# An LSTM's x*Wx+b is copied into the gates' PSUM banks by ScalarE, in place of a bf16 split on GpSimd and products by an identity

## What is computed

```
ys = cond / 16
d  = rsqrt(sum_i (ys*ys) (w*w) + 1e-8)
x  = x + ((x * ys) @ w) * d

xW = x @ Wx + b                     # all steps at once
for each step t, with h = cond and c = 0 before the first:
    a = xW[t] + h @ Wh              # 4 gates of 256: i, f, o, g
    c = sigmoid(f) * c + sigmoid(i) * tanh(g)
    h = sigmoid(o) * tanh(c)
    out[t] = x[t] + h
```

## Time and profile before

| | |
|---|---|
| median of 3 executions | 2039.84 us (2039.63 to 2040.46) |
| the profiled execution, its own time | 2039.63 us |
| its span, from the first to the last instruction | 2037.8 us |
| TensorE products | 1993.6 us busy (98%), 59,057 instructions |
| TensorE weight loads | 1771.2 us (87%) |
| VectorE | 1283.8 us (63%) |
| ScalarE | 747.2 us (37%) |
| GpSimd | 623.1 us (31%) |

### The profile page before, as it was taken

How to read it: one execution, slowest core, us unless ns; L and a number is a source line. 1 busy time by engine, 2 the same in 40 slices (tenths; PEclk the granted TensorE clock), 3 DMA queues, 4 the chain that set the end, 5 groups by cost and what they waited for, 6 DMA issues and landing times.

```text
span 2037.8 us, 146916 instructions
## 1 busy us (share of the span) xinstructions
PE 1993.6 (98%) x59057; PEld 1771.2 (87%) x59057; DVE 1283.8 (63%) x8393; ACT 747.2 (37%) x4239; POOL 623.1 (31%) x1800
## 2 busy tenths in 40 slices
PE   8999999999999999999999999999999999999998
PEld 6888888888888888888888888888888888888887
DVE  6666666666666666666666666666666666666665
ACT  3333333333333333333333333333333333333333
POOL 2332333233333323332332333233333323332332
PEclk9555555555555555555555555555555555555555
DMA  2111011111111111111111111111111110111010
GB/s 95 21 21 27 20 20 25 22 20 21 27 20 20 23 24 20 21 27 20 20 21 27 20 20 26 21 20 21 27 20 20 23 24 20 21 27 20 20 21 20
DMA packets 188304, 48.63 MB, mean 24 GB/s; under 512 B 185468, under 2 KB 187784, under 8 KB 188296
## 3 DMA queue, kind: packets, MB, share of 16 engines
...
...
## 4 chain that ended last, share of the span: by engine, by line
PE 91%; DVE 4%; ACT 2%; issue 2%; DMA 1%; SPq 0%; POOL 0%; POOLq 0%; DVEq 0%
PE psum L386 91%; DVE psum L709 3%; ACT scan_in L785 2%; DMA wx_sb<-in_L_cond_Wx_dram 1%; DVE psum L702 1%; DVE wmax L623 0%; SPq L203 0%; POOL wx_sb L315 0%; DVE xt L602 0%; SPq L205 0%; SPq L198 0%; SPq L199 0%; POOLq L61 0%; PE psum L432 0%; POOL y_cols L308 0%
## 5 line engine op out<-in xcount | busy, mean ns | idle before, releaser
L386 PE MATMUL psum<-h_parts,wh_p 128*128 128x2 f16 (+1 forms) x45056 | 1369.1, 166 | 0.0
L386 PEld LDWEIGHTS psum<-h_parts,wh_p 128*128 128x128 f16 x45056 | 1285.1, 104 | 48.3
L386 PE MATMUL psum<-ring,ident_b 128*128 128x4 bf16 (+2 forms) x12288 | 634.3, 168 | 32.8 <-DVE psum L677 2.6
L386 PEld LDWEIGHTS psum<-ring,ident_b 128*128 128x128 bf16 x12288 | 487.7, 105 | 199.2 <-DVE psum L709 179.3
L782 ACT ACTIVATE sig_f<-psum 128x4 f32<-128x4 f32 x1024 | 178.1, 174 | 1035.4 <-DVE psum L700 1035.4
L700 DVE TENSOR_REDUCE psum<-psum 128x4 f32<-128x8 f32 x1024 | 179.0, 175 | 386.7 <-PE psum L386 386.7
L386 PE MATMUL psum<-x_piece,wx_piece 128*128 128x128 bf16 x1536 | 411.0, 268 | 0.0
L287 POOL CAST ring<-xw 128x64 bf16 (+1 forms) x256 | 121.6, 475 | 906.3 <-POOLq L353 906.1
L712 DVE SCALAR_TENSOR_TENSOR h_parts<-scan_h 128x4 f16<-128x4 f32 x1024 | 174.8, 171 | 247.8 <-ACT scan_h L789 247.8
L787 ACT ACTIVATE scan_h<-psum 128x4 f32<-128x4 f32 x1024 | 180.3, 176 | 141.8
L715 DVE TENSOR_TENSOR_SCAN h_parts<-scan_h,h_parts 128x12 f16<-128x12 f32 x1024 | 188.4, 184 | 35.0
...
## 6 DMA issues: line engine op xcount, KB each, us to landing
x_piece<-x_p SPq DMA_DIRECT2D x128, 192.0 KB, 2.7
wx_piece<-wx_p SPq DMA_DIRECT2D x128, 128.0 KB, 2.4
out_dram<-y_rows SPq DMA_DIRECT2D x512, 4.0 KB
...
small_rows<-in_cond_dram SPq DMA_DIRECT2D x1, 2.0 KB
```

What stands on the lines that cost most here:

```text
L386: return nc.tensor.matmul(out_, lhs, rhs, start=first, stop=last, skip_group_check=True)
```

## The change

ScalarE copies x*Wx+b of the next step, in fp32, from `xw` straight to the gates' PSUM banks, and TensorE's h products add to it. Five copies a step: F after the sigmoid of I and G; I, G and O's two chunks after tanh. F, G and O's first chunk have two sums side by side, one for each part of h; each gets half (`share`, a factor of 0.5 in scale and bias of these items when `xw` is made, by `top`, `units`, `bias_s`). The 12 products by the identity, `ring`, and GpSimd's split of `xw` are gone. TensorE waits for the copies by four semaphores of their own (`f_add`, `i_add`, `g_add`, `o_add`). GpSimd's split of x is spread over the first five steps of a turn, each of its instructions after a step's h, and the SP queue waits for `x_split` one turn less. In the last step of a turn the copies are those of the next turn's first step, and their place is worked out there.

```diff
+        ahead_i = banks[I_BANK][:, sums]
+        ahead_f = banks[F_BANK][:, 0:2 * CB].rearrange("p (c q b) -> p c q b", q=2, b=B)
+        ahead_g = banks[G_BANK][:, 0:2 * CB].rearrange("p (c q b) -> p c q b", q=2, b=B)
+        ahead_o = [banks[O_BANK][:, 0:2 * B].rearrange("p (q b) -> p q b", b=B), banks[O_REST][:, 2 * CB:2 * CB + B]]
...
+        f_add, i_add, g_add, o_add = sem("f_add"), sem("i_add"), sem("g_add"), sem("o_add")
...
-                sp.wait_ge(x_split, i + 2)
+                sp.wait_ge(x_split, i + 1)
...
-            def split_rest(half, src):
-
-                nc.gpsimd.tensor_tensor(by_gate(rest[:, :, :]), src, parts(half, 0), ALU.subtract).then_inc(s_pool, 1)
-                settle()
...
-            def split_low(half):
-
-                nc.gpsimd.tensor_tensor(parts(half, 2), by_gate(rest[:, :, :]), parts(half, 1), ALU.subtract).then_inc(ring_full, 1)
...
-            for s, v in last_read("xw"):
-                pool.wait_ge(s, v)
-            pool.wait_ge(s_start, 1)
-            for half in range(2):
-                src = xw_source(half, 0)
-                split_high(half, src)
-                split_rest(half, src)
-                split_middle(half)
-                split_low(half)
...
+                after_step(t + 1)
+                nc.gpsimd.tensor_copy(part[0], now).then_inc(s_pool, 1)
+                settle()
+                after_step(t + 2)
+                nc.gpsimd.tensor_tensor(res, now, part[0], ALU.subtract).then_inc(s_pool, 1)
+                settle()
+                after_step(t + 3)
+                nc.gpsimd.tensor_copy(part[1], res).then_inc(s_pool, 1)
+                settle()
+                after_step(t + HALF)
+                pool.wait_ge(y_turned, i + 1)
                 pool.sem_inc(pool_seen, 1)
-                for half in range(2):
-                    done = t + (half + 1) * HALF
-                    src = xw_source(half, i + 1)
-                    pool.wait_ge(ring_used, 1)
-                    pool.sem_inc(ring_used, -1)
-                    split_high(half, src)
-                    split_rest(half, src)
...
-                    split_low(half)
-                    after_step(done)
...
-                    save(half, t + half * HALF)
-                    if half == 0:
-                        nc.gpsimd.tensor_copy(part[0], now).then_inc(s_pool, 1)
-                        settle()
-                        nc.gpsimd.tensor_tensor(res, now, part[0], ALU.subtract).then_inc(s_pool, 1)
-                        settle()
-                        nc.gpsimd.tensor_copy(part[1], res).then_inc(s_pool, 1)
-                        settle()
-                        nc.gpsimd.tensor_tensor(part[2], res, part[1], ALU.subtract).then_inc(x_split, 1)
+                save(0, t)
+                after_step(t + HALF + 1)
+                nc.gpsimd.tensor_tensor(part[2], res, part[1], ALU.subtract).then_inc(x_split, 1)
+                after_step(t + UNROLL)
+                save(1, t + HALF)
...
-            def input_apart(gate, u, first, last):
-
-                columns = apart(gate, first, last)
-                mm(columns.rearrange("p c q b -> p q c b"), ident_b[:, :],
-                   ring[:, u, gate, 0:2, B * first:B * last].rearrange("p q (c b) -> p q c b", b=B), True, True)
-                return mm(columns[:, :, 0, :], ident_b[:, :], in_ring(gate, u, 2, first, last), False, True)
-
-            def input_together(gate, bank, u, first, last):
-                for part in range(3):
-                    mm_ = mm(together(bank, first, last), ident_b[:, :], in_ring(gate, u, part, first, last), part == 0, True)
-                return mm_
...
-                    if u % HALF == 0:
-                        pe.wait_ge(ring_full, 2 * i + u // HALF + 1)
                     if u == FIRST_PIECE:
                         pe.wait_ge(x_staged, 32 * i + 32)
                         pe.wait_ge(x_read, i + 1)
-                    pe.wait_ge(f_act, t + u + 1)
-                    input_apart(GATE_F, u, 0, K)
                     if u >= FIRST_PIECE:
                         project(done)
                         done += 1
-                    pe.wait_ge(c_done, t + u + 1)
-                    input_apart(GATE_G, u, 0, K)
-                    input_together(GATE_I, I_BANK, u, 0, K)
-                    pe.wait_ge(o_act, t + u + 1)
-                    input_apart(GATE_O, u, 0, 1)
-                    last = input_together(GATE_O, O_REST, u, 1, K)
-                    if u % HALF == HALF - 1:
-                        last.then_inc(ring_used, 1)
                     if u >= FIRST_PIECE:
                         last = project(done)
                         done += 1
                         if done == len(terms):
                             last.then_inc(x_mm, 1)
+                    pe.wait_ge(f_add, t + u + 1)
+                    pe.wait_ge(i_add, t + u + 1)
                     pe.wait_ge(h_hi, t + u + 1)
                     products(GATE_I, I_BANK, 0, 0, K)
                     pe.wait_ge(h_lo, t + u + 1)
                     products_apart(GATE_F, 0, K).then_inc(f_mm, 1)
+                    pe.wait_ge(g_add, t + u + 1)
                     products_apart(GATE_G, 0, K).then_inc(g_mm, 1)
                     products(GATE_I, I_BANK, 1, 0, K).then_inc(ig_in, 1)
+                    pe.wait_ge(o_add, t + u + 1)
                     products_apart(GATE_O, 0, 1).then_inc(o0_mm, 1)
                     products(GATE_O, O_REST, 0, 1, K)
                     products(GATE_O, O_REST, 1, 1, K).then_inc(o_in, 1)
...
+            nc.vector.scalar_tensor_tensor(out=bias_s[:, :], in0=small[:, B * K:NSMALL], scalar=scales[:, 0:1], in1=share[:, :],
+                                           op0=ALU.mult, op1=ALU.mult).then_inc(s_bias, 1)
+            nc.vector.tensor_scalar(top[:, :], share[:, :], scales[:, 0:1], None, ALU.mult).then_inc(s_bias, 1)
+            link(nc.vector.tensor_tensor(x_unit[:, :], scales[:, 0:1], scales[:, 3:4], ALU.mult))
+            nc.vector.tensor_scalar(units[:, :], share[:, :], x_unit[:, :], None, ALU.mult).then_inc(s_bias, 1)
...
+            def in_two(source, gate):
+
+                return source[:, gate * K:(gate + 1) * K, :].unsqueeze(2).broadcast_to([P, K, 2, B])
+
+            def add_f(source):
+                nc.scalar.activation(ahead_f, in_two(source, GATE_F), ACT.Copy).then_inc(f_add, 1)
+
+            def add_i(source):
+                nc.scalar.activation(ahead_i.rearrange("p (c b) -> p c b", b=B), source[:, GATE_I * K:(GATE_I + 1) * K, :], ACT.Copy).then_inc(i_add, 1)
+
+            def add_g(source):
+                nc.scalar.activation(ahead_g, in_two(source, GATE_G), ACT.Copy).then_inc(g_add, 1)
+
+            def add_o(source):
+                first = GATE_O * K
+                nc.scalar.activation(ahead_o[0], source[:, first, :].unsqueeze(1).broadcast_to([P, 2, B]), ACT.Copy)
+                nc.scalar.activation(ahead_o[1], source[:, first + 1, :], ACT.Copy).then_inc(o_add, 1)
+
+            for s, v in last_read("xw") + last_read("x1"):
+                act.wait_ge(s, v)
+            act.wait_ge(s_start, 1)
+            for add in (add_f, add_i, add_g, add_o):
+                add(step_columns(0, 0))
+
             with act.Fori(0, NI) as i:
                 t = i * UNROLL
+                block = act.snap((i // ITEMS) * ITEMS)
+                column = act.snap((i % ITEMS) * UNROLL)
+                next_block = act.snap((((i + 1) % NI) // ITEMS) * ITEMS)
+                next_column = act.snap(((i + 1) % ITEMS) * UNROLL)
                 item = act.snap((i + LEAD) % NI)
                 chunk = act.snap((item // B) % M)
                 for u in range(UNROLL):
@@ -783,16 +746,26 @@
 
                     act.wait_ge(ig_in, both)
                     nc.scalar.activation(sig_ig, pre_ig, ACT.Sigmoid, scale=unscale).then_inc(cell_in, 1)
+                    if u == UNROLL - 1:
+                        act.wait_ge(x_read, i + 1)
+                        source = step_columns(next_block, next_column)
+                    else:
+                        source = step_columns(block, act.snap(column + u + 1))
+                    add_f(source)
                     act.wait_ge(o_in, both)
                     nc.scalar.activation(scan_h[:, :, 1].rearrange("p (h b) -> p h b", b=B), pre_o, ACT.Sigmoid, scale=unscale).then_inc(o_act, 1)
                     act.wait_ge(c_done, step)
                     nc.scalar.activation(scan_h[:, :, 2], cell[:, :, 2], ACT.Tanh).then_inc(t_done, 1)
+                    add_i(source)
+                    add_g(source)
+                    act.wait_ge(o_act, step)
+                    add_o(source)
                     if u == UNROLL - 1:
 
                         act.wait_ge(x_mm, i + 1)
                         act.sem_inc(act_seen, 1)
                         nc.scalar.activation(xw[:, bass.ds(item, 1), :].rearrange("p n t -> p (n t)"), banks[X_BANK][:, 0:P], ACT.Identity,
```

(2 more changed lines are left out.)

58 lines of the change are left out of this document (16 added, 42 removed).

## The result

| | before | after |
|---|---|---|
| median | 2040.15 us (4 executions, 2039.63 to 2040.68) | 2111.97 us (4, 2111.66 to 2112.51) |
| ratio | | 1.0352 (95%: 1.0334 to 1.037) |
| the profiled execution, its own time | 2039.63 us | 2111.66 us |
| its span | 2037.8 us | 2109.9 us |
| first to last of F's sums (L700, now L631) | 1987.12 us | 2057.39 us |

The forecast was 2109, with 2066 to 2128 as its range.

A forecast was written before the change was run, and what follows sets the result against it. The prediction took a chain of 1,024 steps as the bound, with TensorE waiting for h. From 2039.6 us, +61.4 (wait), -13.3 (GpSimd's stall) and +21.1 (ScalarE's copies) gave 2108.8, so 2109 us, range 2066 to 2128.

The forecast's parts named there:

- The wait: Ahead of the h products: waiting for h_hi, i_add and f_add costs 0.06 us more a step, +61.4 us.
- the rival of the cheap wait: Ahead of the h products: the extra wait costs only 0.02, as at L635; 2073 us, chance 0.09.
- GpSimd's stall: Scan L709 held by GpSimd's subtraction L292 once a turn; spreading the split removes this, -13.3 us.
- The last subtraction of x: GpSimd, following the saving of y: ends about when or before L709 starts, so no new collision is booked.
- ScalarE's copies: Address calculations and copies delay tanh in a turn's eighth and first steps: 0.165 us a turn, +21.1 us.
- Steps 2 to 7: ScalarE within a turn: copies, 0.13 apart, finish before the sigmoid of O, h and the next sigmoid; cost 0.
- The turn's end: ScalarE's copies and X-bank copy end at tanh + 1.29, when the next sigmoid is wanted; cost 0.
- The identity products: TensorE, 12 a step: they lie in the hole where h is being made, so removing them gains 0.
- The start: Ahead of the loop: extra VectorE and ScalarE work against 12 fewer identity products, under 1 us, taken as 0.
- The forecast's own range: Whole kernel: 2095 to 2125 us, allowing for rounded rows and an eighth step costing 0.05 to 0.25; chance 0.72.
- The rival of a free wait: Ahead of the h products: the wait costs nothing and only ScalarE's eighth step hurts; 2055 us, chance 0.06.

The follow-up runs named there:

- e6: Changed kernel with only the order of the three names ahead of the h products altered to f_add, h_hi, i_add: 2064.41 us, ratio 1.0112.
- e7: Changed kernel with h_hi named first in source, so the h load itself waits for h: 2048.65 us, ratio 1.0036.
- e5_split_placed: Kernel before, with each piece of GpSimd's work released by a given step's h and SP waiting for x_split one turn less: 2030.98 us, ratio 0.9952.
- e8_registers: Changed kernel with ScalarE's next block and column worked out in the seventh step and kept in registers: 2095.76 us, ratio 1.0265.
- e10_turn_end: Changed kernel with h_hi named first, block and column registers set in the seventh step, X-bank copy's addresses in the sixth: 2031.51 us, ratio 0.9959.
- e9: Changed kernel with h_hi named first and ScalarE's block and column registers worked out in the seventh step: 2040.3 us, ratio 0.9997.
- e3_filler: Changed kernel with ten identity products a step, into an unread bank, while h is being made: 2111.63 us, ratio 1.0357.
- e1: Changed kernel with a TensorE semaphore increment between the copies' waits and h's, so the h load waits for h_hi alone: 2047.08 us, ratio 1.004.

## Why the prediction was right

The time was right to 3 us, and so were the mechanisms. That it is so close is in part luck: the wait was 6 us dearer than forecast, the copies and the stall together 5 us better, and 2 us came from the start.

- **The wait: +61.4 predicted, +67.6 in the trace** (66 ns x 1,024). The gap rose by 63 ns where I had 60; the rest lies behind the load, from where F's sum comes after 636 ns and not 631, for a cause that stays open. The source of the number, the two loads of 0.11 and 0.12 in the earlier trace rows, was the right one, and the reason given for preferring them, that the late name comes first there as `h_hi` does, is what e6 and e7 showed. That the extra wait is an instruction of its own on the path was argued there; the row of L471 shows it. The prediction took this for a likeness and not for the rule. The rule would have closed the rival of the cheap wait, for L635's late name stands second.
- **GpSimd's stall: -13.3 predicted.** The fourth step lost 109 ns a turn, 14.0 us, and e5_split_placed gets 13.9 out of the loop of the kernel before with the same means. The mean less the median of the earlier trace rows was the right reading. The last subtraction of x did not meet the scan: no scan of after is above 192 ns. The eighth step's 12 ns, the cast beside L715, went too, 1.5 us that I had not seen.
- **ScalarE's copies: +21.1 predicted, +18.9 in the trace** (124 + 24 = 148 ns x 128). I had 165 ns. The F copy starts 0.40 behind the sigmoid of I and G in the eighth step and 0.30 in the first, as I took it. From it to tanh it is 0.17, near the 0.18 of the sum, though in other parts: 0.12 to the sigmoid of O and 0.05 from there to tanh, where I had 0.09 twice. So tanh is late by 133 and 33 ns, which is the forecast. What I missed is that a tanh so close behind another activation takes 167 ns and not 175, so that h is late by 124 and 24 only. e8_registers gives the eighth step's part back whole, and in e10_turn_end the first step's is gone too.
- **Steps 2 to 7: 0.** Right, with one wrong size: the F copy comes 0.18 behind the sigmoid and not 0.13; its address row (126 ns) is longer than those of the copies behind tanh (43 to 46). The sigmoid of O at 1007.70 was still on time. Behind tanh the copies are 0.10 to 0.12 apart.
- **The turn's end: 0.** Right, by 0.08: the X-bank copy ends at 1011.18 and the sigmoid starts at 1011.26. It was right only because the eighth step and the wait were late, as the prediction said of the wait. e8 and e9 took this cover away, and the end cost 31 and 91 ns a turn.
- **The identity products: 0.** e3_filler shows it.
- **The start: 0.** Between the two profiled executions it is 1.6 us, but hardly of the change: e1 and e3, with nearly the same code up to there, have their first F sum at 44.0 and 44.5, the kernel before at 44.4 (below).

The forecast's own range (2095 to 2125) held it. The rival of a free wait would have been nearly right for the same change with its names in another order (e7_h_first: 2048.65; the rival gave 2055).

So the change is not slower by its idea. Two accidents of writing cost all of it: which name the h load carries, and where ScalarE works out its addresses. With both mended, and the turn's end with them, the same change is 0.6% faster than the kernel before. What it gains is GpSimd's stall.
